# Token lists of an expert layer: counting and one-hot products inside the attention stage, in place of a selection stage

## The reference

```
logits = x @ gate_w.T; probs = softmax(logits)        # 8192 x 32
topk_w, topk_idx = top_k(probs, 4)                    # then normalised
e_flat = topk_idx.reshape(-1); t_flat = repeat(arange(t), 4)
order = argsort(e_flat)                               # by expert, in token order
pos = arange(t * K) - starts[e_s]                     # rank within the expert
slot = minimum(pos, C)                                # C = 128 slots, the rest is dropped
buf[e_s, slot] = x[t_s]; ... expert_out; routed.at[t_s].add(expert_out * gate)
```

## Time and profile before

| what | us |
|---|---|
| three runs | 2113.36, 2090.95, 2110.30 (median 2110.3) |
| the profiled execution | 2094.39, span 2092.3 |
| stage 1 | 9 to 244 |
| selection stage | 244 to 359 |
| expert stage | 359 to about 486 |
| Mamba stage and last layer | from there to the end |

### The profile page before, as it was taken

The page is one execution under the profiler, slowest core; times in us unless marked ns, Lnnn a source line. Parts: engine busy times, 40 slices in busy tenths (PEclk is TensorE's granted clock), DMA queues, the critical chain, the costliest instruction groups (busy, mean ns, idle before and its releaser), DMA issues.

```text
span 2092.3 us, 22136 instructions
## 1 busy us (share of the span) xinstructions
...
## 2 busy tenths in 40 slices
...
GB/s 152 110 108 108 130 220 25 39 42 28 152 77 106 117 117 113 55 117 75 107 117 117 94 74 105 85 140 107 6 85 115 47 42 189 237 175 219 168 201 74
DMA packets 215243, 229.75 MB, mean 110 GB/s; under 512 B 24456, under 2 KB 182216, under 8 KB 210760
## 3 DMA queue, kind: packets, MB, share of 16 engines
...
...
## 4 chain that ended last, share of the span: by engine, by line
PE 34%; issue 20%; DVE 18%; another core or an unknown queue 9%; ACT 6%; POOL 4%; SPq 4%; DMA 3%; DVEq 1%; POOLq 0%; ACTq 0%
PE bank L1208 11%; DVE hst L1557 10%; PE bank L1163 5%; PE bank L1073 2%; DMA wv<-packed_weights 2%; PE bank L1161 1%; PE bank L1296 1%; PE bank L1313 1%; PE bank L1197 1%; SPq L583 1%; PE bank L1221 1%; PE bank L1299 1%; PE bank L1175 1%; PE bank L1322 1%
## 5 line engine op out<-in xcount | busy, mean ns | idle before, releaser
L1557 DVE TENSOR_TENSOR_SCAN hst<-bank,dbx 128x512 f32<-128x512 f32 x512 | 591.8, 1205 | 44.1 <-ACT bank L949 40.2
L752 POOL TENSOR_TENSOR dbx<-u,ball 128x1024 f32<-128x1024 f32 x256 | 617.8, 2497 | 4.8 <-POOL u L783 2.8
L1208 PE MATMUL bank<-prod,ident 128*128 128x512 f32 x1024 | 501.9, 625 | 32.6 <-DVE prod L1573 27.5
L949 ACT ACTIVATE bank<-dt,aneg 128x511 f32<-128x511 f32 x512 | 347.7, 688 | 309.6 <-DVE hst L1557 309.0
L1208 PEld LDWEIGHTS bank<-prod,ident 128*128 128x128 f32 x1024 | 201.9, 199 | 247.7 <-issue 196.5
L1573 DVE TENSOR_TENSOR prod<-hst,bank 128x1024 f32<-128x1024 f32 x192 | 233.5, 1216 | 18.2 <-DVE hst L1557 14.8
L814 POOL DMA_INDIRECT yg<-expert_rows,row_of x128 | 124.2, 970 | 167.4 <-DMA expert_rows<-yu 111.0
L761 POOL TENSOR_TENSOR prod<-hst,call 128x1024 f32<-128x1024 f32 x64 | 161.1, 2517 | 60.3 <-DVE hst L1557 60.2
L1597 DVE SCALAR_TENSOR_TENSOR hg<-bank,wv,ha 128x256 f32<-128x256 f32 x96 | 42.1, 479 | 154.1 <-ACT ha L1002 80.7
L1192 PE MATMUL bank<-parts,sel_c 128*128 128x512 bf16 x152 | 59.6, 394 | 105.5 <-DVE prod L1573 104.8
L647 POOL TENSOR_SCALAR rstd<-mv 128x4 f32<-128x4 f32 x16 | 3.7, 230 | 198.7 <-DVE mv L1377 198.7
...
## 6 DMA issues: line engine op xcount, KB each, us to landing
...
```

The costliest lines, as they stand in the source:

```text
L752: gp.tensor_tensor(dbx[n % NDB][:, :, :], u[s.par][:, :, :], ball[:, n:n + 1, :].to_broadcast([P, NH, SEQ]), ALU.mult).then_inc(dbx_rdy, 1)
L949: act.activation(da_ps[h][:, 1:SEQ], dt_[s.par][:, h, 1:SEQ], ACT.Exp, scale=aneg[:, h, n:n + 1]).then_inc(da_rdy, 1)
L1208: last = mm(y_ps[:, h, :], ident[:, :], from_[:, h, :], start=False, stop=(n == NS - 1), skip_group_check=True)
L1557: dve.tensor_tensor_scan(h_of[:, h, :], da_ps[h][:, :], dbx[n % NDB][:, h, :], 0.0, ALU.mult, ALU.add).then_inc(scan_rdy, 1)
```

## The change

The stage 1 functions take a third argument: in one pass they serve the attention of sequence `a`, the router of `r = a - 1` and the lists of `l = a - 2`. The table in memory, its loads and the two rounds of `take` are gone. In their place:

- PE adds up, from the bf16 mask and triangular and all-ones matrices, the rank of each token within each expert in this sequence (`rank_ps`; tokens not chosen get a large negative number) and the totals (`tot_ps`): 12 products in place of 4 transposes.
- DVE adds the totals so far (`carry`) and splits the rank into a slot row of 16 (`rka`) and a slot column of 8 (`rkb`): six small instructions after the normalisation.
- POOL subtracts the numbers 0 to 7 and 0 to 15 from them (`dgb` of 128x1024 and `dga` of 128x2048, bf16), DVE compares with zero (`ohb`, `oha`), and ACT scales `ohb` by row and tile numbers (`ohv`).
- PE multiplies: 4 tiles, 4 groups of 8 experts and 2 values, 32 bf16 products of 128x128 by 64 into the free half of bank 3 (`list_ps`), and DVE adds the result to `lsum`.
- After the last sequence a short tail picks out each expert's own entries (`lx`, `ll`), turns them twice on PE and makes `idx`.

The order of the work on the engines that wait for each other:

On DVE, the end of one pass and the head of the next, in the kernel before (a row names the line, the operation, the tile written and those read, and the size).

The diff, cut to its core:

```
-            mask = eb("mask", [P, TT, E0])
+            mask = eb("mask", [P, TT, E0], BF16)
...
+            dga = eb("dga", [P, TT * E0, SLOT_A], BF16)
+            dgb = eb("dgb", [P, TT * E0, SLOT_B], BF16)
+            oha = eb("oha", [P, TT, E0, SLOT_A], BF16)
+            ohb = eb("ohb", [P, TT, E0, SLOT_B], BF16)
+            ohv = [eb(f"ohv{v}", [P, TT, E0, SLOT_B], BF16) for v in range(2)]
...
+        rank_ps, tot_ps, list_ps = bank[4][:, 0:TT * E0], bank[4][:, TT * E0:TT * E0 + E0], bank[3][:, 256:512]
...
-                sp.wait_ge(maskT_rdy, s.at(1, 1))
-                settle(sp)
-                sp.dma_start(mask_d[:, bass.ds(s.at(SEQ), SEQ)], maskT[:, :]).then_inc(st_m, 16)
...
-            sp.wait_ge(st_m, NB * 16)
-            for k in range(NSEG):
-                sp.dma_start(val[k * E0:(k + 1) * E0, :], mask_d[:, k * SEG:(k + 1) * SEG]).then_inc(seg_loaded, 16)
...
+            def digit_off(dst, digit, width, done):
+                a = digit[:, :].rearrange("p (k w) -> p k w", w=1).to_broadcast([P, TT * E0, width])
+                b = iota_e[:, 0:width].rearrange("p (k w) -> p k w", k=1).to_broadcast([P, TT * E0, width])
+                gp.tensor_tensor(dst[:, :, :], a, b, ALU.subtract).then_inc(done, 1)
+
+            def slots_of(s):
+
+                gp.wait_ge(rank0, s.at(6, 6))
+                need(gp, ohb_rdy, s.at(1))
+                settle(gp)
+                digit_off(dgb, rkb, SLOT_B, dg_rdy)
+                need(gp, oha_rdy, s.at(1))
+                digit_off(dga, rka, SLOT_A, dg_rdy)
...
             rsqrt(rstd, mv, Seq(0, 0), mv_rdy, rstd_rdy)
+            rsqrt(rstd, mv, Seq(0, 1), mv_rdy, rstd_rdy)
+            slots_of(Seq(0, 0))
             with gp.bass.Fori(0, NB // 2 - 1, engines=(gp.engine,), hint_back_edge=True) as j:
-                for i in (1, 2):
+                for i in (2, 3):
                     rsqrt(rstd, mv, Seq(j, i), mv_rdy, rstd_rdy)
-            rsqrt(rstd, mv, Seq(0, NB - 1), mv_rdy, rstd_rdy)
-
-
-            make(gp.memset(upper[:, :], 1.0))
-            make(gp.affine_select(out=upper[:, :], in_=upper[:, :], compare_op=ALU.is_ge, fill=0.0, base=-1,
-                                  pattern=[[1, P]], channel_multiplier=-1))
-            make(gp.memset(onesb[:, :], 1.0))
+                    slots_of(Seq(j, i - 1))
+            slots_of(Seq(0, NB - 1))
...
-                    act.wait_ge(mt_mm, r.at(1, 1))
-                    need(act, st_m, r.at(16))
-                    act.activation(maskT[:, :], kva_ps[0:E0, :], ACT.Copy).then_inc(maskT_rdy, 1)
...
+                if l:
+                    act.wait_ge(ohb_rdy, l.at(1, 1))
+                    need(act, list_mm, l.at(1))
+                    settle(act)
+                    act.activation(ohv[0][:, :, :, :], ohb[:, :, :, :], ACT.Identity, scale=row_no[:, 0:1]).then_inc(ohv_rdy, 1)
+                    for k in range(TT):
+                        act.activation(ohv[1][:, k, :, :], ohb[:, k, :, :], ACT.Identity, scale=tile_no[:, bass.ds(l.at(TT, k), 1)]
+                                       ).then_inc(ohv_rdy, 1)
...
+                    need(pe, rank0, r.at(6, -4))
...
-                    need(pe, maskT_rdy, a.at(1, -1))
+                    need(pe, list_sum, a.at(1, -2))
...
+                    chosen = mask[:, :, :].rearrange("p t e -> p (t e)")
+                    mm(rank_ps, upper[:, :], chosen, start=True, stop=False, skip_group_check=True)
+                    mm(rank_ps, negbig[:, :], chosen, start=False, stop=False, skip_group_check=True)
+                    for k in range(TT - 1):
+                        for later in range(k + 1, TT):
+                            mm(rank_ps[:, later * E0:(later + 1) * E0], onesb[:, :], mask[:, k, :], start=False, stop=(k == TT - 2),
+                               skip_group_check=True)
+                    for k in range(TT):
+                        last = mm(tot_ps, onesb[:, :], mask[:, k, :], start=(k == 0), stop=(k == TT - 1), skip_group_check=True)
+                    last.then_inc(mt_mm, 1)
+                if l:
+                    pe.wait_ge(ohv_rdy, l.at(5, 5))
+                    pe.wait_ge(oha_rdy, l.at(1, 1))
                     pe.wait_ge(kvx_rdy, a.at(1, 1) if a else NB)
                     for k in range(TT):
-                        last = pe.transpose(kva_ps[0:E0, tile(k)], mask[:, k, :], ident[:, :])
-                    last.then_inc(mt_mm, 1)
-
-            stage1(Seq(0, 0), None)
+                        for g in range(GROUPS):
+                            of_g = slice(g * EXPERTS, (g + 1) * EXPERTS)
+                            for v in range(2):
+                                last = mm(list_ps[:, g * 64:(g + 1) * 64], oha[:, k, of_g, :].rearrange("p e a -> p (e a)"),
+                                          ohv[v][:, k, of_g, :].rearrange("p e b -> p (e b)"), start=(k == g == v == 0), stop=(k == TT - 1), skip_group_check=True)
+                    last.then_inc(list_mm, 1)
...
+            pe.wait_ge(list_rdy, 2)
+            for g in range(GROUPS):
+                last = pe.transpose(bank[6][0:SLOT_B, tile(g)], ll[:, g, :], ident[:, :])
+            last.then_inc(idx_mm, 1)
...
+            for k in range(SLOT_A):
+                last = mm(bank[5][:, 0:E0], sel_s[:, k, :], lt[:, :].rearrange("b (n a) -> b n a", a=SLOT_A)[:, :, k],
+                          start=(k == 0), stop=(k == SLOT_A - 1))
+            last.then_inc(idx_mm, 1)
...
+                    dve.wait_ge(dg_rdy, l.at(2, 1))
+                    need(dve, ohv_rdy, l.at(5))
+                    ts(ohb[:, :, :, :].rearrange("p t e b -> p (t e) b"), dgb[:, :, :], 0.0, None, ALU.is_equal).then_inc(ohb_rdy, 1)
...
+                    dve.wait_ge(dg_rdy, l.at(2, 2))
+                    need(dve, list_mm, l.at(1))
+                    ts(oha[:, :, :, :].rearrange("p t e a -> p (t e) a"), dga[:, :, :], 0.0, None, ALU.is_equal).then_inc(oha_rdy, 1)
...
+                    dve.wait_ge(mt_mm, r.at(1, 1))
+                    tt(rnk[:, :].rearrange("p (t e) -> p t e", t=TT), rank_ps.rearrange("p (t e) -> p t e", t=TT),
+                       carry[:, :].rearrange("p (t e) -> p t e", t=1).to_broadcast([P, TT, E0]), ALU.add).then_inc(rank0, 1)
+                    dve.wait_ge(rank0, r.at(6, 1))
+                    tt(carry[:, :], carry[:, :], tot_ps, ALU.add).then_inc(rank0, 1)
+                    ts(rkt[:, :], rnk[:, :], 1.0 / SLOT_B, 0.5 / SLOT_B - 0.5, ALU.mult, ALU.add).then_inc(rank0, 1)
+                    dve.wait_ge(rank0, r.at(6, 3))
+                    ts(rkt[:, :], rkt[:, :], MAGIC, None, ALU.add).then_inc(rank0, 1)
+                    dve.wait_ge(rank0, r.at(6, 4))
+                    need(dve, dg_rdy, r.at(2))
+                    ts(rka[:, :], rkt[:, :], MAGIC, None, ALU.subtract).then_inc(rank0, 1)
+                    dve.wait_ge(rank0, r.at(6, 5))
+                    stt(rkb[:, :], rka[:, :], -float(SLOT_B), rnk[:, :], ALU.mult, ALU.add).then_inc(rank0, 1)
+                if l:
+                    dve.wait_ge(list_mm, l.at(1, 1))
+                    need(dve, list_sum, l.at(1))
+                    tt(lsum[:, :], lsum[:, :], list_ps, ALU.add).then_inc(list_sum, 1)
...
-            tt(val[:, :], val[:, :], rev[:, :], ALU.mult).then_inc(taken, 1)
-            dve.wait_ge(taken, 1)
-            take(val[:, :], cand, cand_rdy)
...
+            dve.wait_ge(list_sum, NB)
+            tt(lx[:, :, :, :].rearrange("p g e b -> p (g e b)"), lsum[:, :], own[:, :, :, :].rearrange("p g e b -> p (g e b)"), ALU.mult
+               ).then_inc(list_rdy, 1)
             dve.wait_ge(list_rdy, 1)
-            tt(idxf[:, :], empty[:, :], first[:, :], ALU.subtract).then_inc(list_rdy, 1)
-            dve.wait_ge(list_rdy, 2)
-            ts(idxf[:, :], idxf[:, :], float(TOK), None, ALU.add).then_inc(list_rdy, 1)
+            dve.tensor_reduce(ll[:, :, :], lx[:, :, :, :].rearrange("p g e b -> p g b e"), AX.X, ALU.add).then_inc(list_rdy, 1)
             dve.wait_ge(idx_mm, 1)
-            dve.tensor_copy(idx[:, :], bank[6][:, 0:E0]).then_inc(list_rdy, 1)
+            dve.tensor_copy(lt[:, :], bank[6][0:SLOT_B, :]).then_inc(list_rdy, 1)
+            dve.wait_ge(idx_mm, 2)
+            ts(empty[:, :], bank[5][:, 0:E0], 0.0, empty_no[:, 0:1], ALU.is_equal, ALU.mult).then_inc(list_rdy, 1)
+            dve.wait_ge(list_rdy, 4)
+            stt(idx[:, :], bank[5][:, 0:E0], -1.0, empty[:, :], ALU.add, ALU.add).then_inc(list_rdy, 1)
```

More of the change, by code:

```diff
@@ L29 @@
 XGW = D + E0
-NSEG = 4
-N_EARLY = 5 + NSEG
-N_CONST = N_EARLY + 16
-SEG = TOK // NSEG
+N_EARLY = 15
+SLOT_A, SLOT_B, EXPERTS = 16, 8, 8
+GROUPS = E0 // EXPERTS
+BIG = 16384.0
+N_CONST = N_EARLY + 15
 DI, NH, NS = 256, 2, 16
@@ L221, in build @@
             rstd = eb("rstd", [P, TT])
-            rev = eb("rev", [P, SEG])
-            val = eb("val", [P, SEG])
-            cand = eb("cand", [P, P])
-            cval = eb("cval", [E0, NSEG * P])
-            first = eb("first", [E0, P])
```

(35 more changed lines are left out.)

87 lines of the change are left out of this document (44 added, 43 removed).

## The result

The changed kernel takes **2093.1 us** (median of 20 runs, 2079.9 to 2103.6) where the kernel before takes 2107.6 (20 runs, 2088.4 to 2125.1) on the same chip: ratio **0.9942, 95% interval 0.9917 to 0.9967**, 0.6% less (the two medians alone give 0.9931; ratios below are the recorded ones, with their intervals). The forecast said 2116, 0.7% more: the time lies inside its range of 2062 to 2148, but on the other side of the kernel before. The experiments ran on other chips, on which the median of both kernels is under 1970 us; each is compared with the kernel before on its own chip. There the changed kernel's ratio is 0.9902 (0.9883 to 0.9921), 19 us less. One execution of the kernel before, beside e6, e7 and e8, took 3048 us and is left out of their ratios.

The account below looks back on a forecast made before the run. Stage 1 was taken as a loop of waits, the selection stage as DVE working alone. 14 longer passes +100 us, tail -89.5 and later stages +3 gave +14, put on 2102: 2116 us, range 2062 to 2148.

Parts of the forecast that it names:

- Rank: Each stage 1 pass, DVE after the normalisation: six dependent small instructions, 1.0 to 1.9 us, taken as 1.6.
- POOL's two instructions: Each stage 1 pass: dgb 2.5 us and dga 5.0, taken as 7.3 together, from 1.7 to 9.0.
- Blocking: Each stage 1 pass: DVE's two-SBUF-input kf and qf wait for whole POOL instructions; maxima start at 10.1 us, not 4.45.
- The back, 10.4: Each stage 1 pass, maxima to the next normalisation's end: oha +0.3 to +0.8 us and PE's clock; +1.1 taken.
- The half clock: PE in the back of a pass: half speed after an idle gap, 0 to +1.5 us in part of the passes.
- Lists off the path while blocking holds: PE in each pass: 32 list products 2.5 us, k and v 1.99; maxima possible at 7.6 to 8.75, before 10.1.
- Tail: From the last normalisation to idx: 37 us (32 to 42) against 126.5, so -89.5 us.
- Expert stage: From idx to Mamba's first load: SP's transfers beside the gathers slow their landing by 0 to 10 us; +3 taken.
- A: Rival for stage 1, chance 0.25: no blocking, front 7.6 to 8.75 us, pass 17.6, in all 2070 us.
- B: Rival for stage 1, chance 0.20: PE at half clock throughout, lists 5 us, pass 22.4, in all 2144 us.
- C: Rival for the expert stage, chance 0.05: transfers hold up gathers and scatters, 4 groups by 5 us, in all 2136.
- The base: Whole kernel before the change: 2102 us, the middle of two pairs of executions, 2091 and 2094, 2110 and 2113.

Follow-up runs that it names:

- e6: The changed kernel, unchanged, run again on another chip beside the kernel before; ratio to the kernel before 0.9902.
- e7: The changed kernel with SP's clearing of sorted_rows issued behind the packing of the weights instead of ahead; ratio to the kernel before 0.9910.
- e8: e2 with the eight kva products on PE done three times over; ratio to the kernel before 0.9918.
- e4: The changed kernel with POOL computing dga twice, one after the other; ratio to the kernel before 1.0192.
- e1: The changed kernel with ACT's Relu written in place in PSUM, so kf and qf have one SBUF input; ratio to the kernel before 0.9822.
- e3: The changed kernel with the edits of e1 and e2, and lsub and mask reading the logits from PSUM; ratio to the kernel before 0.9589.
- e10: The kernel before with the edit of e1 (Relu in place in PSUM); ratio to the kernel before 1.0005.
- e2: The changed kernel with PE running k, v and q of the next sequence ahead of the 32 list products; ratio to the kernel before 0.9962.
- e5: The kernel before, unchanged, profiled once more on another chip; span 1964.0 us, ratio 1.
- e9: The changed kernel with dgb in fp32 instead of bf16; one run, no ratio given, pass 17.94 us.

## Why the prediction was wrong

Of 14 passes the forecast said +100 us, and they were +64; everything else up to Mamba's first load came out within 3 us. The mechanism of the pass, blocking by POOL, was right; its length was not. By its own steps:

1. **Rank**, 1.6 us on DVE: done 1.41 after the normalisation (100.81), POOL starts at 1.67 as said (1.7). Right.
2. **POOL's two instructions, "I take 7.3 for both"**: 6.04 (101.07 to 107.11). This is the step that failed. The nearest row, `dbx` at 2497 ns for 1024 results, was taken for instructions of another kind of input, and 7.3 overstates them by a fifth. Since POOL's time enters the pass one for one (e4), 1.26 us are 18 us in all. The Trainium skill (GPSIMD Engine Reference, § 3.1 Elementwise) with 4.5 us for 2048 was nearer to the measured 3.66 to 4.17 than the doubled row's 5.0, and still above it. And 4.12 is not all POOL's own: `dga` takes 3.67 us in every pass of e1 and e3, and 4.12 in the pass shown, where it begins at 102.99 while `kf` still runs to 103.58; it waits 0.45 for DVE as DVE waits for it.
3. **Blocking**: right, in mechanism and place. The maxima start 0.47 after `dga` ends; I had them 1.1 after POOL's end at 9.0, so 0.6 us a pass (8 us) too much. e1, e3 and e10 show that what is blocked is an instruction whose inputs are in SBUF: with one input in PSUM `kf`, `qf`, `lsub` and `mask` run at full speed beside the same POOL instruction. The Trainium skill (SBUF — State Buffer, § Who interferes with whom) has the rule for the pair; the runs extend it from AFFINE_SELECT to POOL's TENSOR_TENSOR.
4. **The back, 10.4**: 9.4 to 9.6 in most passes and 9.65 in the mean, against 9.30 before. `oha`, put at +0.3 to +0.8, cost 0.1 to 0.3 together with all else. The half clock that I put on the back came in these traces only after a long idle stretch on PE; I had it between 8 and 11.8, 3.8 us, and with the shorter front it was 1.0 to 2.7 in all passes but two. In one of these it was 3.97 (251.62, shown with e2), the granted clock 0.50 and the back 10.69, as I had it; in e2 the stretch is 3.8 or more in every pass, and the back 10.8. So most of the term hung on point 2, and fell with it: another 0.75 us a pass, 10 us or so.
5. **Lists off the path while blocking holds**: right, but narrowly. The products were faster than said (1.1 to 1.9 us against 2.5), k and v mostly slower (2.0 to 3.8 against 2.0; the 3.36 of the pass shown had a granted clock of 0.58), and the maxima can start at 7.3 (e1) where the forecast had 7.6 to 8.75: PE's path lay only 1 us below POOL's, which is why freeing `kf` and `qf` alone saved 1.1 to 1.3 us a pass.

**Tail**: 37.2 against 37, by two errors that cancel. The list products took 1.9 us (4.5 forecast) and POOL was done 1.5 earlier; the 16 small fp32 products at the end took 7.03 of a chain that was to last 5.5 in all and took 9.5. **Expert stage**: +5.6 on the first chip and +5.3 on the other, against +3. With the measured terms the forecast's own sum is 64 - 89 + 5 = -20. Up to Mamba's first load the first chip shows -20.0, and the others -13.6 (e6 against e5) to -21.9 (e9 against e10), as the pass of the kernel before varies from 13.10 to 13.43.

Of the rivals, A had the right sign for another reason; its condition, no blocking, does not hold, and with `kf` and `qf` freed (e1) the pass is 16.8, below A's 17.6. (A's "17.8 at most" was added up wrongly, too: 8.75 and 9.8 are 18.55.) B's trigger did come, list products at the low clock (114.65 us, granted 0.52) and k and v mostly so, but not its price: the list products took 1.84 there and not 5, so PE's path stayed below POOL's. C's 20 us did not come: the expert stage grew by 4.3 (e9 against e10) to 5.6 in all. The base flatters the forecast by luck: I took 2102 for the kernel before, and its median is 2107.6. So 2116 is only 23 us off, while the difference, +14 forecast and -15 measured, is 29 off.
